# A four-layer network's last layer: the mixture's dispatch in one run on GpSimd's queue, more answer buffers, a later gate

## What is computed

```python
# the mixture (inside the attention block, last of its steps)
out = out + cw[:, e:e + 1] * ((silu(flat @ W1[e]) * (flat @ W3[e])) @ W2[e])
# the feed-forward
h = _swiglu(t @ w1 + b1)          # min/clip at 7, sigmoid, times (lin + 1)
acc = acc + we[:, None] * (h @ w2 + b2)
# the end of the layer
x = x + s * silu(ffn)
```

## Time and profile before

| | |
|---|---|
| median of 3 runs | 923.76 us (917.67 to 923.87) |
| span of the profiled execution | 921.0 us |
| PE, DVE, ACT, POOL busy | 75%, 65%, 43%, 32% |
| mean granted clock of PE | 0.870 |

### The profile page before, as it was taken

One profiled execution on the slowest core, in us unless ns is written; L12 is line 12 of the kernel. 1 busy time (PEld: TensorE's weight loads), 2 busy tenths in 40 slices (PEclk: granted clock), 3 DMA queues, 4 the chain that ended last, 5 costly groups with the idle time before them and its releaser, 6 DMA issues. The chain is left out here.

```text
span 921.0 us, 14463 instructions
## 1 busy us (share of the span) xinstructions
PE 692.4 (75%) x4255; PEld 516.3 (56%) x4255; DVE 595.3 (65%) x1590; ACT 399.3 (43%) x990; POOL 292.5 (32%) x303
## 2 busy tenths in 40 slices
PE   4999866743979379328986988999976677749991
PEld 2999834632767248327875674656544444426560
DVE  4797487538688611286667567889947665636685
ACT  3201334534735123164444446767756333326660
POOL 1373143540000265300100002445410555665552
PEclk9999878865799779768997899999997699969996
DMA  9991001220100140319008431222100122112515
GB/s 286 244 281 77 1 27 44 68 69 0 47 0 1 11 47 9 93 51 391 1 1 156 124 86 34 75 78 73 53 25 17 48 61 60 57 54 57 163 58 141
DMA packets 79564, 72.97 MB, mean 79 GB/s; under 512 B 9618, under 2 KB 73885, under 8 KB 78977
## 3 DMA queue, kind: packets, MB, share of 16 engines
q1 hardware_dynamic: 68000, 57.56, 23.3%
q0 software_dynamic: 7072, 12.40, 5.2%
q10 hardware_dynamic: 4416, 2.10, 0.9%
HBM read 42.85 MB, written 27.46 MB: 76 GB/s over the span
## 5 line engine op out<-in xcount | busy, mean ns | idle before, releaser
L3493 POOL DMA_INDIRECT ys<-work,back_to x78 | 78.9, 1011 | 83.7 <-DVE work L3452 38.0
L3336 PE MATMUL banks<-weights,work 128*128 x156 | 91.6, 673 | 7.8 <-issue 6.2
L2535 DVE TENSOR_REDUCE work<-banks 128x2 f32<-128x512 f32 x128 | 83.5, 683 | 14.4 <-PE banks L2526 13.1
L3349 PEld LDWEIGHTS banks<-consts,work 128*128 128x128 f32 x156 | 21.8, 155 | 79.4 <-issue 52.5
L3359 PE MATMUL banks<-weights,work 128*128 x312 | 54.8, 303 | 5.4 <-DVE work L3452 3.2
L3349 PE MATMUL banks<-consts,work 128*128 128x128 f32 x156 | 34.3, 305 | 32.1 <-DVE work L3441 15.5
L816 POOL DMA_INDIRECT xs<-t,idx x48 | 49.1, 1023 | 28.7 <-DMA ys<-work,back_to 15.4
L2526 PE MATMUL banks<-work 96*128 96x256 bf16 x256 | 49.3, 277 | 9.1 <-DVE work L2535 6.0
L1196 POOL DMA_INDIRECT g<-rows,back_to x16 | 15.3, 958 | 120.4 <-DVE back_to L1922 115.8
L3359 PEld LDWEIGHTS banks<-weights,work 128*128 128x128 f32 x312 | 46.2, 213 | 8.1 <-issue 7.7
L2939 PE MATMUL banks<-work 99*128 99x256 bf16 x256 | 48.7, 275 | 1.7 <-issue 1.6
(11 more groups left out here) (508 smaller groups left out, 1946.1 us busy)
## 6 DMA issues: line engine op xcount, KB each, us to landing
weights<-in_w SPq DMA_DIRECT2D x1, 6668.0 KB, 19.6
weights<-in_w SPq DMA_DIRECT2D x1, 4569.5 KB, 33.8
work<-xs SPq DMA_DIRECT2D x62, 64.5 KB
weights<-in_r SPq DMA_DIRECT2D x1, 2950.5 KB, 26.5
xs<-zero SPq DMA_DIRECT2D x1, 2600.0 KB, 26.1
xs<-zero SPq DMA_DIRECT2D x1, 2580.0 KB, 33.5
work<-xs SPq DMA_DIRECT2D x39, 65.0 KB
weights<-in_w SPq DMA_DIRECT2D x1, 2124.5 KB, 12.1
```

The costliest lines, as they stand in the source:

```text
L2535: v.tensor_reduce(self.mxb[:, 2 * h:2 * h + 2], self.n.bank(bank).rearrange("p (r n) -> p r n", r=2), AX, ALU.max, negate=True).then_inc(* ...
L3336: pe.matmul(self.mid(t), self.hT[t % 4], w1[:, bass.ds(off * 4, 512)], start=True, stop=True).then_inc(*self.prod1.up())
L3349: ins = pe.transpose(self.mid(m)[:, 128 * f:128 * f + 128], self.ha[m % 4][:, 128 * f:128 * f + 128], self.c["ident"])
L3493: g.indirect_dma_start(ys[:, :], bass.IndirectOffsetOnAxis(ap=n.back_to[:, t:t + 1], axis=0), self.yb[t % self.RETURNS], None, bounds_chec ...
```

## The change

Four things. `RETURNS` goes from 28 to 40 buffers of 128 columns; the 12 new ones lie in the weights of the third layer, which are no longer used. The number of semaphores for landed answers stays 7. POOL issues answers 0 and 1 and then the whole dispatch, 32 sends with the wait and the two small operations in their middle, before answer 2. The waits after every second answer are gone; what is left from answer 14 on is a wait for the pair of answers that lies seven pairs back. The gate's `pause` goes from 2 to 17 rounds, and the loads of the feed-forward's answers from round `FFN` + 16 to `FFN` + 22.

```diff
-    FFN, TILES, RETURNS, SEND, AHEAD = 39, 78, 28, 2, 3
+    FFN, TILES, RETURNS, SEND, AHEAD = 39, 78, 40, 2, 3
-        self.row_out = [n.sig(f"expert_back{u}", 16) for u in range(self.RETURNS // 4)]
+        self.row_out = [n.sig(f"expert_back{u}", 16) for u in range(7)]
-            ... (6912, C, self.RETURNS)))
+            ... (6912, C, 28)))
+        spare = n.w2.tensor
+        self.yb += [spare[:, C * i:C * i + C] for i in range(self.RETURNS - 28)]
         for t in range(self.TILES):
-            if t >= self.SEND:
-                take(send, 2)
+            if t == self.SEND:
+                for _ in send:
+                    pass
             if t % 2 == 0 and t >= 2 * len(self.row_out):
                 g.wait_ge(*self.returned(t // 2 - len(self.row_out)))
...
-            if t % 2 and self.SEND <= t < self.SEND + NT:
-                g.wait_ge(*self.sent.sent.at(2 * (t - self.SEND) + 1))
-                g.wait_ge(*self.returned(t // 2))
...
-    gate = FfnGate(n, ffn_rows, ffn_got, sent2.done(), 32, 2)
-    n.run(Opening(n, norm, n.turn, mix, experts), gate, Later(ffn_got, experts.FFN + 16))
+    gate = FfnGate(n, ffn_rows, ffn_got, sent2.done(), 32, 17)
+    n.run(Opening(n, norm, n.turn, mix, experts), gate, Later(ffn_got, experts.FFN + 22))
```

More of the change, by code:

```diff
@@ L3239, in setup @@
         self.rows, self.hT, self.ha, self.hm, self.at_, self.yb = (
-            cut(*x) for x in ((0, C + 2, 8), (1040, C), (1552, 512), (4096, 512), (6144, 256, 3), (6912, C, self.RETURNS)))
+            cut(*x) for x in ((0, C + 2, 8), (1040, C), (1552, 512), (4096, 512), (6144, 256, 3), (6912, C, 28)))
         self.at_ += cut(3600, 256, 1)
+        spare = n.w2.tensor
+        self.yb += [spare[:, C * i:C * i + C] for i in range(self.RETURNS - 28)]
     def ffn(self, t):
```

## The result

The changed kernel takes 938.25 us, the median of four runs (935.09 to 941.65), beside 923.82 us for the kernel before, measured with it. The ratio is 1.0198, 95% interval 1.0157 to 1.0239. The prediction was 924.0 us with a range of 904 to 935; the result lies outside.

The account below looks back on a forecast made before the run. It took PE's completions, late when POOL issues indirect DMAs 1.3 us apart for about 9 us, as the source of the stops. Span 921.0 - 1.6 (feed-forward) + 1.7 (gate) = 921.1, median 2.8 above: 924 us, range 904 to 935.

Parts of the forecast that it names:

- POOL's timetable: Dispatch on POOL: two runs of 16 sends at 1.31 us, 722.5 to 743.5 and 746.3 to 767.2, answers following without pause.
- The lock-out of GpSimd by DVE: POOL's sends during DVE-heavy work: DVE may shut GpSimd out of ports; were all sends 1.19 us, two runs some 6 us longer.
- The share s: Feed-forward tiles: part of each POOL run after its first 9 us lost to PE's lateness; 0.5 taken, answer 38 1.6 us earlier.
- rival 2: Feed-forward tiles: PE stands until POOL has caught up (s = 1), answer 38 10.2 us later, 935.7 us; chance with worse 0.22.
- the clean pace: Feed-forward tiles on DVE without stops: 2.34 us each, read from answers 16 to 21.
- The gate's relief of the mixture's tiles: Mixture: 15 tiles rid of gate pieces take 1.635 instead of 1.745 us each, 1.7 us gained.
- The gate's pieces at the end: Behind the last answer on DVE: 19 gate pieces take 11.9 us, 8.5 hidden, 3.4 stick out.
- an L3706 that waits for a DMA: Sign at the kernel's end that the forecast is wrong: it would mean POOL's answers end later than thought.
- The buffers: Answer buffers: twelve more are worth nothing and cost nothing.
- The sum: Whole kernel: 921.0 - 1.6 + 1.7 = 921.1 us of span, median 2.8 us above it, so 924 us, no change.
- Rival 1: Feed-forward tiles: no long stops (s = 0), 26.9 us gained, 1.7 lost, 898.6 us; chance 0.15.
- the earlier end of the dispatch: Dispatch over at 769, not 802, so SP can load the mixture's rows then; worth nothing by itself.

Follow-up runs that it names:

- The run alone: The changed kernel with gate and feed-forward answer loads back as before, leaving the run of sends and 40 buffers; ratio 1.0105 to the kernel before.
- chip D: Chip of the last runs, kernel before 885.4 us there: the change again, ratio 0.9869, and the change without later gate, mixture's answers spaced, no ratio.
- the distances in the mixture alone: The change without its later gate, with a small clearing on POOL ahead of answers 39 to 75 only; ratio 0.9868 where the kernel before takes 881.7 us.
- with 1.37 us up to answer 59: The change without its later gate, one small-tile clearing ahead of each POOL send and answers 2 to 59; ratio 1.0074 to the kernel before.
- chip A: Chip of the first follow-ups, kernel before 918.2 us there: gate only 1.0034, run of sends and 40 buffers only 1.0105.
- chips C and D: Chips of the last follow-ups, where the kernel before takes 881.7 and 885.4 us; the change has ratio 0.9869 on the second.
- the first pair: The change measured together with the kernel before on the first chip: 938.25 beside 923.82 us, ratio 1.0198.
- chips A and B: Chips of the earlier follow-ups, where the kernel before takes 918.2 us on the first, 922.1 and 914.9 us on two occasions on the second.

## Why the prediction was wrong, step by step

**POOL's timetable** was right: the last send of the first run stands at 743.02 (its end was said for 743.5), the second begins at 746.86 (746.3) and its last send is at 766.14 (767.2 was to be its end). The lock-out of GpSimd by DVE that the prediction had weighed beside it left no mark: the 32 sends took 0.990 us in the mean, 1.006 before. (The page of the Trainium skill that it had cited for this, SBUF — State Buffer, "SBUF: two separate sides", limits the case of two SBUF inputs to a GpSimd operation that reads SBUF, which the prediction left out.)

**The share s** is the step that failed. I took 0.5 between 0.27 and 0.84. It was 1: between the ninth microsecond of the first run, 732.4, and its end nothing was written but what came out at 746.42, and from 756.41, nine microseconds into the second, to 777.59 nothing either. That is rival 2, and its own figures fit: POOL caught up at 776.6 by it, at 776.44 in the trace; answer 38 at 845.8 by it, at 843.50 in the trace, earlier because the free tiles took 2.24 us (answer 12 at 785.39 to answer 38 at 843.50), not 2.34. The stretch costs 7.1 us where I had -1.6, so this term is 8.7 of the 15.1 us by which the sum was short. That s = 0.84, which I kept as the upper bound, also gives 7.1 is luck: the true share was higher and the free tiles were quicker. The mistake was to average two rows of unlike kind. The run of 15 answers was the same code in the same stage. The first layer's run was other work, which asks less of PE's semaphores: 18 rises are due in its 22 us, and a tile at the clean pace needs four in 2.34 us. If they come through one at a time, the stage that needs more of them loses more. By the nearest row the sum would have been 921.0 + 7.1 + 1.7 + 2.8, 933 us.

**The gate's relief of the mixture's tiles**, -1.7 us, came out as +3.0 (65.87 to 68.83), and is the second term that failed. The gate isn't to blame: alone it gave 65.1. The run alone gave 68.4. In the change POOL's answers leave in threes (848.96, 850.25, 851.70; 854.54, 855.82, 857.11; 860.17), and DVE's idle time before the first of each three is 1.6 to 2.2 us. On chip D, without the hold, the same tiles take 62.1 us and the gaps are gone. The late rises are there, too: of 107 recorded ones in the change's mixture tiles 20 come 0.5 to 1.4 us late, and in 847 to 865 us there is one of over a microsecond at about every third answer; of as many in before's tiles it is 4, on chip D none. So the loss goes with the hold. What was to test the groups of three, the distances in the mixture alone, ran only where there was nothing to lift; with 1.37 us up to answer 59, on chip A, the tiles took 66.6 instead of 68.4, which fits. That the groups of three are what makes these rises late stays argued, not shown. Where neither has the hold, something like the predicted relief is seen: 63.6 us with the early gate (and the distances), 62.1 with the later one.

**The gate's pieces at the end**: +3.4 predicted, +4.4 measured. The 19 pieces took 12.2 us, from the end of the last answer at 912.68 to 924.83, where I had 11.9. The rest, 0.7 us, is a wait that I missed: ACT issues half of the last loads from its own queue, at 922.39, behind the last activation of the gate, which the change moved behind the last answer; SP's half went at 916.34. L3706 waits 0.71 us for it. I had named an L3706 that waits for a DMA as a sign that POOL's answers end late. POOL's last answer left at 914.18, 1.9 us behind DVE's; it was the queue of the loads.

**The buffers** showed no worth, as said.

**The sum** of the measured terms: +0.8 up to answer 5, which the prediction had at nothing, +7.1, +3.0, +4.4, together 15.2 us of span (unrounded), 921.0 to 936.2. Rival 2 stood at 935.7 for the median, which was measured at 938.25; its chance was 0.22. That it came so near is part luck: its stretch was 3.1 us too long, and it had the mixture's tiles 4.7 and the end 1.0 us too short.

**Rival 1**, no long stops, is what happens on chips C and D: 0.9869 there for the change and 0.9868 without its later gate, against 0.973 by its sum. The gain is smaller because the kernel before won't have those stops there either, but the wait before answer 32, some 12 us, for the mixture's rows. (It has no trace from these chips; this is read from the one with its answers spaced.) There the earlier end of the dispatch, which the prediction had at nothing, is what the change gains. The prediction treated the hold as a property of the kernel to be read from one trace. It goes with where, or when, it runs: the kernel before takes 914 to 924 us in the first pair and on chips A and B, and 882 to 885 on C and D.

For rival 2 I had cited the Trainium skill (NOTIFIC — the notification-queue block, "Overflow: three behaviours"): full queues of the block, which carries the records of traces, push back on the engines. The length of the stands agrees with such a push-back. But no run here shows a queue, and on chips C and D 40 transfers 1.27 to 1.3 us apart hold nothing. One thing points to the recording itself. Of 1075 rises of PE's semaphores the traces with the hold have 908 to 962, the six without it 1065 to 1069. Every execution timed here was a recorded one, so no run tells how much of the hold, or of the difference between the chips, a kernel that isn't recorded would see. The cause of the hold stays open. So does whether it belongs to the chip or to its condition at the time: the runs came on six occasions, the four with the hold before the two without it, and only B was met twice.

## What to carry to other kernels

When a trace shows waits that end with "remote" on a kernel of one core, find out what they go with, and time the kernel on more than one chip before tuning around them: here one change is 2% worse where they are and 1.3% better where they aren't. If the recording of the trace may be what delays an engine, a time without it is needed; here there is none. Where the hold is there, GpSimd's indirect transfers in groups of four with a stop between let TensorE's completions through, but count whether GpSimd can afford the stops: of the kernels here that had them none was faster than the kernel before, clear of the noise. And when work is moved behind the last tile, look at what the same engine's queue was to issue there.

## What the runs showed of the hardware

- With GpSimd issuing indirect transfers of 128 rows 1.27 us apart, a completion of TensorE's reached DVE 13 us after its modelled end, and DVE stood still for 9.7 and 15.1 us, until GpSimd stopped. TensorE's semaphores rose in order, one at a time and 3 to 10 us apart as far as recorded, and the arrears within 0.13 us once GpSimd had stopped. Over 33 tiles the loss was as large at 1.37 us (108.9 us), and there was none at 1.63 us (73.3). A stop every 4, 6, 8 transfers: 77.8, 89.6, 102.7 us, 109.6 without. With 16 instead of 130 columns a row: 110.9.
- The hold was met in the first pair and on chips A and B, and not on C and D. GpSimd's pace (0.97 us a transfer and 0.30 us of issue) was the same on both kinds. Where it was absent, answer 5 of the same program was already 19 us (before, up to there) and 25 us (the change) earlier. So it seems to cost time in the earlier layers too: one wait of 12.3 us on "remote" (L1186, DVE) of the change's trace is missing in its trace on chip D.
- The clock fell in the stands. In 739 to 746 us of the change PE did nothing, and the granted clock was 0.50, the lower level (1.2 GHz). Over 732 to 782 us it was 0.62 in the mean with PE busy for a third of the time, and 1.00, the upper level (2.4 GHz), in the same window where PE was busy for nine tenths (chip D, and 1.63 us on chip B).
